# The first group's row maxima move from the attention stage into the last chunk of the projections

## The reference

```python
x = x + 0.5 * ffn(layernorm(x))      # 1024 -> 1024 product with bias, 8 LoRA experts of rank 16, 2 chosen per token
x = x + attn(layernorm(x))
x = x + 0.5 * ffn(layernorm(x))

# attn: 32 query heads of 32, 8 key/value heads, so 4 query heads share one key head
q, k, v = resid @ Wq, resid @ Wk, resid @ Wv
q, k = rope(q), rope(k)
att = einsum('bhgqd,bhkd->bhgqk', q, k) / sqrt(32)      # causal mask, then softmax over the keys
out = (softmax(att) @ v) @ Wo
```

## Time and profile before

| | us |
|---|---|
| three runs | 1561.04, 1562.6, 1565.38 (median 1562.6) |
| the profiled execution, its time | 1565.67 |
| the profiled execution, its span in the trace | 1563.9 |
| TensorE busy in the span | 1511.8 (97%) |
| VectorE, ScalarE, GpSimd busy | 958.9, 569.3, 693.0 |
| mean granted clock of TensorE | 0.984 of full |

### The profile page before, as it was taken

How to read it: one execution, slowest core, us unless ns; L and a number is a source line. 1 busy time by engine, 2 the same in 40 slices (tenths; PEclk the granted TensorE clock), 3 DMA queues, 4 the chain that set the end, 5 groups by cost and what they waited for, 6 DMA issues and landing times. The chain is left out here.

```text
span 1563.9 us, 25960 instructions
## 1 busy us (share of the span) xinstructions
PE 1511.8 (97%) x9184; PEld 1197.1 (77%) x9184; DVE 958.9 (61%) x2727; ACT 569.3 (36%) x1057; POOL 693.0 (44%) x382
## 2 busy tenths in 40 slices
PE   8899998999999969999999999999999999999999
PEld 7899998888888845555555555555479999999998
DVE  6545454656463468888888888888645434343433
ACT  4233232221121125565665565556633212121210
POOL 1222222533343415888888888888612101010100
PEclk9999999999999969999999999999999999999999
DMA  6322324342322262344333333440152212121201
GB/s 232 124 98 110 121 99 148 127 146 81 122 95 81 104 141 63 94 98 97 88 77 76 76 76 89 102 102 28 54 205 79 81 41 81 42 80 40 80 14 41
DMA packets 118773, 145.95 MB, mean 93 GB/s; under 512 B 40976, under 2 KB 77072, under 8 KB 118384
## 3 DMA queue, kind: packets, MB, share of 16 engines
q1 hardware_dynamic: 89920, 120.52, 26.7%
q10 hardware_dynamic: 28736, 23.93, 4.7%
HBM read 95.66 MB, written 53.51 MB: 95 GB/s over the span
## 5 line engine op out<-in xcount | busy, mean ns | idle before, releaser
L1540 ACT ACTIVATE at_probs<-ps 128x512 f32<-128x512 f32 (+1 forms) x640 | 308.1, 557 | 148.3 <-PE ps L1450 147.5
L1609 DVE CUSTOM_DVE_ANT_0 ps<-ps,at_score_mask 128x512 f32<-128x512 f32 (+3 forms) x512 | 289.9, 621 | 50.7 <-PE ps L1439 49.7
L321 POOL TENSOR_TENSOR f_x_ring<-f_x_ring,f_half_bias 128x1024 f32<-128x1024 f32 x32 | 78.1, 2444 | 308.0 <-DVE f_h L607 303.1
L1379 POOL TENSOR_TENSOR at_added<-at_added,at_probs 128x2048 f32<-128x2048 f32 (+1 forms) x60 | 210.8, 3513 | 2.2
L1439 PE MATMUL ps<-at_ks,at_qs 96*128 96x512 f32 (+3 forms) x528 | 185.5, 377 | 16.0 <-DMA at_ks<-scr_k_hi 10.8
L1450 PE MATMUL ps<-at_qs,at_ks 98*128 98x512 f32 (+3 forms) x528 | 178.4, 376 | 3.8 <-ACT at_probs L1540 3.0
L1450 PEld LDWEIGHTS ps<-at_qs,at_ks 98*128 98x128 f32 x528 | 96.6, 193 | 89.9 <-ACT at_probs L1540 50.4
L1465 PE MATMUL ps<-at_probs,at_vs 128*32 128x512 f32 (+3 forms) x1536 | 156.2, 494 | 0.0
L48 PE MATMUL f_ps<-f_wt_hi,f_hT_hi 128*128 128x400 f32 (+1 forms) x384 | 134.4, 350 | 3.3 <-DVE f_hT_lo L611 3.3
L1439 PEld LDWEIGHTS ps<-at_ks,at_qs 96*128 96x128 f32 x528 | 101.4, 197 | 41.7 <-issue 11.2
L50 PE MATMUL f_ps<-f_wt_hi,f_hT_lo 128*128 128x400 f32 (+1 forms) x384 | 131.7, 343 | 0.0
(11 more groups left out here) (164 smaller groups left out, 3159.4 us busy)
## 6 DMA issues: line engine op xcount, KB each, us to landing
at_qs<-scr_q_hi SPq DMA_DIRECT2D x20, 512.0 KB, 5.8
f_x_ring<-in_L_attn_resid SPq DMA_DIRECT2D x16, 512.0 KB, 3.6
x<-f_x_ring SPq DMA_DIRECT2D x16, 512.0 KB, 2.7
early<-x SPq DMA_DIRECT2D x16, 512.0 KB, 3.3
scr_q_hi<-qkv_rope_hi ACTq DMA_DIRECT2D x32, 256.0 KB, 2.0
scr_q_lo<-qkv_rope_lo ACTq DMA_DIRECT2D x32, 256.0 KB, 2.3
scr_ctx<-at_ctxn SPq DMA_DIRECT2D x32, 256.0 KB, 2.4
shared<-scr_ctx SPq DMA_DIRECT2D x16, 512.0 KB, 4.5
```

Source lines behind the costliest of these rows:

```text
L321: pool.tensor_tensor(x_ring[:, u, :], x_ring[:, u, :], half_bias[:], ALU.add).then_inc(bias_added, 1)
L1379: pool.tensor_tensor(added[:, heads, :], first, probs[:, (NU * n + u) % PROBS, heads, :], ALU.add).then_inc(added_done, 1)
L1540: act.activation(probs[:, (NU * n + u) % PROBS, g, cols], score_ps[x % BANKS][:, cols], ACT.Exp, scale=SCALE).then_inc(exp_done, 1)
L1609: dve.tensor_tensor_reduce(out=src, in0=src, in1=mask, scale=1.0, scalar=part_max[:, g, own] if c else -3.0e38, op0=ALU.add, op1=ALU.max, ...
```

## The change

- The 48 row items and the two turns of group 0 are made in the last chunk of `qkv_stage`. PE puts one item behind each of the weight rows c = 1 to 6 of outputs 2 to 9 (six items per output, seven where the turn stands among them). DVE takes the maxima of output o+1's items after its work for output o. Turn B stands ahead of the second value tile. The slots are PSUM banks 0, 1, 6 and 7.
- For that, SP loads the queries and keys of group 0 (and the keys, later the queries, of group 1) within the stage, once the value tiles of the third chunk are done, and writes the rows of maxima of group 0.
- The queries and keys lie where attention will read them: `heads` is an array that both stages hold (it carries the high and low parts of the even chunks' activations before), and group 1's queries lie in the second half of the low query weights, which become `wo`'s low part later. `wq` and `wo` share the pair `wide`.
- The raw weight ring `wkv_raw` shrinks from 4 to 2 slots, and `rot` gets an array of its own.
- ACT takes one exponential of `eps` at the end of `qkv_stage`.
- Attention starts with the eight scores of units 0 and 1 of group 0. The special branches for group 0 are gone; the 49 items of group 1 are spread over units 0 to 8 of group 0 by the rule that holds for the other groups.

```diff
+ROWS = [("row", i, g, c) for i in range(NQ) for c in range(i // QH + 1) for g in range(G)]
+TURN_A, TURN_B = ("turn", 0), ("turn", 1)
+TURN_AT = QH * G + G
...
-    WRAW = 4
+    WRAW = 2
+    ROW_FROM, ROW_SLOTS, PER_O = 2, 4, 6
...
+        hT = sb("hT", [P, 2, KC, HALF], F32R)
+        hT_hi, hT_lo = [[heads[:, part, :, :], hT[:, part, :, :]] for part in range(2)]
...
-        rot = early[:, 3, :].rearrange("p (a n) -> p a n", n=HALF)
+        rot = sb("rot", [P, 2, HALF], F32)
...
+        q_stacks = [hT_hi[0], flat(wq_lo)[:, KC * HALF:].rearrange("p (b n) -> p b n", n=HALF)]
+        behind = hT_lo[0].rearrange("p c n -> p (c n)")
+        k_stacks = [behind[:, n * T:(n + 1) * T] for n in range(3)]
+        spare = flat(wkv_raw)
+        score_mask = spare[:, 0:MASK]
...
+        slot_ps = [ps[:, bank, :] for bank in (0, 1, 6, 7)]
+        items = ROWS[:TURN_AT] + [TURN_A] + ROWS[TURN_AT:] + [TURN_B]
+        number = {it: q for q, it in enumerate(items)}
...
+            own = ROWS[(o - ROW_FROM) * PER_O:(o - ROW_FROM + 1) * PER_O] if ROW_FROM <= o < NO else []
+            return [it for row in own for it in ([TURN_A, row] if row == ROWS[TURN_AT] else [row])]
...
+            def load_negative(half):
+                sp.wait_ge(row_read, number[(TURN_A, TURN_B)[half]] + (ROW_SLOTS + 1))
+                for row, src in enumerate((neg_hi, neg_lo)):
+                    dst = q_stacks[0][KROWS + row:KROWS + row + 1, half * G:(half + 1) * G, :].rearrange("p g t -> p (g t)")
+                    sp.dma_start(dst.bitcast(F32), src).then_inc(neg_loaded, 16)
...
+            sp.wait_ge(v_done, (B * NCH - 1) * TC + 1)
+            for s in range(2):
+                sp.wait_ge(out_stored[s], NCH * NO * 16 + 16)
+            sp.wait_ge(wkv_lo_done, KC)
+            load_queries(0, first_head_loaded)
+            load_keys(0, first_head_loaded)
+            sp.dma_start(score_mask[:, HALF:MASK], consts["score_mask"]).then_inc(first_head_loaded, 16)
+            load_keys(1, rest_loaded)
+            load_negative(0)
+            sp.wait_ge(proj_done, (B * NCH - 1) * NO + KC)
+            load_queries(1, rest_loaded)
+            load_negative(1)
+            sp.wait_ge(rest_loaded, 6 * 16)
+            sp.wait_ge(neg_loaded, 4 * 16)
...
+            def row_item(it):
+                q = number[it]
+                if q == 0:
+                    pe.wait_ge(first_head_loaded, 7 * 16)
+                    pe.wait_ge(v_copied, (B * NCH - 1) * TC + 2)
+                pe.wait_ge(row_read, q + (ROW_SLOTS if it == TURN_B else 1))
+                out = slot_ps[q % ROW_SLOTS]
+                if it[0] == "turn":
+                    pe.transpose(out[0:G * QH, 0:P], row_max[:, it[1], :, :].rearrange("p g q -> p (g q)"),
+                                 ident[:]).then_inc(row_filled, 1)
+                    return
+                _, i, g, c = it
+                keys = row_keys(i, c)
+                pe.matmul(out[:, 0:keys], q_stacks[0][0:KROWS, i // QH * G + g, (i % QH) * P:(i % QH + 1) * P],
+                          k_stacks[0][0:KROWS, c * HALF:c * HALF + keys], start=True, stop=True).then_inc(row_filled, 1)
...
+                        own = [] if more else items_of(o)
...
+                            if 1 <= c <= len(own):
+                                row_item(own[c - 1])
...
+                    if not more and s < 2:
+                        pe.wait_ge(row_read, len(items) - 1 + ROW_SLOTS)
+                    if not more and s == 1:
+                        row_item(TURN_B)
...
+            def negative(half):
+                q = number[(TURN_A, TURN_B)[half]]
+                act.wait_ge(row_filled, q + 1)
+                if half:
+                    act.wait_ge(neg_loaded, 2 * 16)
...
+                    if not more and o and TURN_A in items_of(o):
+                        negative(0)
...
+                    if not more and s == 1:
+                        negative(1)
...
+            act.activation(std[:], eps[:], ACT.Exp)
...
+                if g == NO:
+                    pool.wait_ge(v_done, (B * NCH - 1) * TC + 1)
+                    pool.memset(score_mask[:, 0:HALF], 0.0).then_inc(mask_ready, 1)
+                    pool.wait_ge(mask_ready, 1)
+                    pool.memset(behind[KROWS:KROWS + 2, 0:3 * T].bitcast(F32), 1.0).then_inc(mask_ready, 1)
+                    pool.wait_ge(mask_ready, 2)
+                chunk_step(B - 1, g)
...
+                    if not more:
+                        for it in items_of(o + 1):
+                            row_item(it)
                 rope_sum(b, ch * NO + NO - 1)
+                if not more:
+                    row_item(TURN_B)
...
+        qs = [in_heads(heads[:, 0, :, :].rearrange("p c n -> p (c n)")),
+              in_heads(shared[:].rearrange("p t a c n -> p (t a c n)")),
+              sb("qs2", [P, 2, G, HALF], F32R)]
+        second = in_heads(flat(wo[1])[:, KC * HALF:])
+        ks = heads[0:KROWS + 2, 1, 0:2 * RING, :].rearrange("p c n -> p (c n)").rearrange("p (r t) -> p r t", t=T)
+        def q_stack(n):
+            return second if n == 1 else qs[n % RING]
...
-            load_k(sp, 0, slice(0, HALF), early_loaded)
-            load_q(sp, 0, slice(G, 2 * G), stacks_loaded[0])
-            load_k(sp, 0, slice(HALF, T), stacks_loaded[0])
-            load_v(0)
-            load_rows(0, 0)
-            load(1)
+            for r in range(2):
+                sp.sem_inc(stacks_loaded[r], LOADS - 16)
+                load_v(r)
+            for stored in ctx_stored:
+                sp.sem_inc(stored, 16)
             for n in range(NG):
-                load_rows(n, 1)
                 if n:
+                    load_rows(n, 1)
                     store(n - 1, 0)
                 if n + 2 < NG:
...
-            pe.wait_ge(const_ready, 3)
-            pe.wait_ge(const_loaded, 16)
...
+                if u == 0:
+                    pe.wait_ge(stacks_loaded[n % RING], n // RING * LOADS + LOADS)
...
-            pe.wait_ge(early_loaded, 6 * 16)
+            for u in range(AHEAD):
+                for g in range(G):
+                    scores(0, u, g)
             for n in range(NG):
                 for u in range(NU):
-                    if n == 0 and u in (0, H0):
-                        half = u // H0
-                        for m, it in BEFORE[half]:
-                            if (m, it) == (0, rows[QH * G]):
-                                pe.wait_ge(stacks_loaded[0], LOADS)
-                            slot_item(m, it, it == TURN_A)
-                        for x, items in enumerate(BETWEEN[half]):
-                            scores(0, u + x // G, x % G)
-                            for m, it in items:
-                                slot_item(m, it)
...
-            load_q(act, 0, slice(0, G), early_loaded)
+            act.sem_inc(exp_done, BANKS)
+            act.sem_inc(ctx_copied, 1)
+            for u in range(AHEAD):
+                for g in range(G):
+                    exps(0, u, g)
             for n in range(NG):
                 for u in range(NU):
-                    if n == 0 and u in (0, H0):
-                        negative(0, u // H0)
-                        for x in range(AHEAD):
-                            for g in range(G):
-                                exps(0, u + x, g)
...
-                    if n == 0 and u in (0, H0):
-                        for m, it in BEFORE[u // H0]:
-                            slot_item(m, it)
-                        for items in BETWEEN[u // H0]:
-                            for m, it in items:
-                                slot_item(m, it)
```

More of the change, by code:

```diff
@@ L1010, in low_part, with chunk_step @@
                                    ALU.subtract).then_inc(lo_done, 1)
[L1012 to L1013 removed]
+            def chunk_step(b, g):
                     cols = slice((g // NO) * HALF, (g // NO + 1) * HALF)
```

171 lines of the change are left out of this document (97 added, 74 removed).

## The result

The changed kernel takes 1550.64 us in the median of five runs (1549.88 to 1554.55), the kernel before 1561.55 (1560.73 to 1565.38): ratio 0.9926, 95% interval 0.9913 to 0.9939, so 10.9 us faster. The forecast was 1551.0, inside a range of 1544 to 1557.

The account below looks back on a forecast made before the run. The prediction took TensorE, busy 97% of the span, as the bound. Savings of 31.0 us less losses of 10.3 and 8.9 gave 11.8 saved: 1550.8 against the 1562.6 median, stated as 1551, range 1544 to 1557.

Parts of the forecast that it names:

- Part 1, attention's start: From PE's end of the values to group 0's closing sums: 42.7 us instead of 73.7, a saving of 31.0.
- The hand-over: Between PE's last value matmul and attention's first score: 4.0 us, from a range of 3.3 to 4.2.
- The clock: At attention's start: probably falls in the idle gap, back when unit 0 begins or little later; 1.5 us, bounds 0 and 5.0.
- the denser mix: In group 0 of attention: group 1's 49 items share nine units instead of ten; 1.2 us more at PE's step.
- Part 2, the last chunk: In the last chunk of the projections: items, turns and two new waits on PE lose 10.3 us.
- The first loads' wait: In the last chunk: the first item waits for seven DMAs, 0 to 3 us, taken as 0.5.
- The last maximum: At the last chunk's end: the first value tile waits for DVE's last maximum, about 0.4 us.
- that rival: In the last chunk: DVE's items do not overlap and set the pace, 4.8 us more, 1556; chance 0.13.
- that of the late loads: In the last chunk: first items' loads land 4 us late, 3.5 more plus 2.5 for the clock, 1557; chance 0.08.
- the prediction's sign: In the changed profile: the last chunk's ten outputs 9 to 10 us longer, no PE wait over 1 us for DVE.
- Part 3, the ring of two: At the projections' start: first tile's turn 6.4 us later, plus 2.5 for restarting at half clock; 8.9 lost.
- one of the signs of being wrong: At the projections' start: PE turning the first tile before 290 would mean the ring costs little.

Follow-up runs that it names:

- busy_scores: The changed kernel with 14 unread matmuls behind the last value tile and one behind each of attention's first eight scores; 1548.76 us, 0.991 of the kernel before.
- short_maxima: The changed kernel with the last chunk's 48 row maxima on VectorE reading 16 keys each, score matmuls whole; 1551.78 us, 0.9926 of the kernel before.
- ring_alone: The kernel before with only the raw weight ring cut from 4 to 2 slots; 1571.58 us, 1.006 of the kernel before.
- heads_low: The changed kernel with `heads` moved to the low end of memory, `early` and `shared` to the high end; 1554.04 us, 0.9944 of the kernel before.

## Why the prediction held, point by point

- **Part 1, attention's start** (42.7 predicted, 42.83 measured). The hand-over is right (4.0, measured 3.89). The clock was mis-sized: 1.5 taken, 3.05 by busy_scores. The text had the clock back when unit 0 begins or a little later; it came back 6.9 us behind the start of unit 0, where half clock is dear. The sum was kept by two terms that were too dear, read in busy_scores at full clock: 4.2 for the eight scores, measured 3.55, and 31.8 + 1.2 from unit 0 to the sums, measured 32.35, so the denser mix costs 0.55 and not 1.2 (group 1 takes 31.80 from its first score, 612.72, to 644.52). So errors of 1.3 and 1.55 us cancel, and the near hit of this part is luck too.
- **Part 2, the last chunk** (10.3 predicted, 10.7 with the value tiles left out). The items' price is right within a fifth: 8.8 predicted for the 48 matmuls, 10.08 measured. All four sizes were put too low, those of 128 columns the most (0.1, measured 0.122). The turns were put at 0.3 each and cost about half of that. The first loads' wait (0.5) did not come, and PE took the first item without idle time. The last maximum was right (0.4, measured 0.43). VectorE does not pace the chunk, by short_maxima: that rival falls, and so does that of the late loads. The outputs grew by 10.7 us and not by 9 to 10, as the prediction's sign had it.
- **Part 3, the ring of two** (8.9 predicted). The front costs 9.2, but the ring's part of it is 6.85 by ring_alone: 5.58 for the first turn (6.4 predicted, with 5.5 as the lower bound) and 1.48 between the first and the second (2.5 for the clock). The other 2.35 is not in ring_alone; heads_low gives back 1.88 of it from the third turn on, so nearly all of it is the place of `heads`, which the prediction did not have at all. The near hit of this sum is luck. By the letter one of the signs of being wrong came true: TensorE turned the tile at 288.38, before 290. But the first transposes came 3.57 us sooner in this execution than in the earlier trace rows; counted from them it is 24.76 us where the sign's 290 stands for 22.8, so the ring is not cheap and the sign was badly put. Besides, the text held that a tile normalized ahead of ACT's eighth piece is what the order forbids. True of this order, but two moved operations undo it and show that the loss is not one of the ring.
- **The sum.** In us from the first transposes: + 9.20 in front, + 10.71 in the last chunk, + 0.16 in the value tiles, - 30.85 from their end to the sums, - 0.30 behind, that is 11.08 saved against 11.8 predicted. The mechanisms of the three parts held; the closeness of the total owes something to errors that cancelled inside the parts.

## What to carry to other kernels

A smaller ring need not cost time, though the wait shows up at once: look at which short operations stand behind the ring's transfers in each engine's order, and move them out, on every engine that the next tile passes through (here ScalarE's, then GpSimd's). When a stage starts with work that a slower engine feeds, the clock can fall inside the start, not only at the border, and a few filler matmuls between the real ones, whose results nobody reads, can keep it up where those at the border alone do not (3.05 us against 0.12 here). Ask too where the half clock falls: it cost next to nothing while TensorE waited for ScalarE, and 0.44 us per microsecond behind that. Compare profiles from a landmark behind the parts that the change does not touch: here one such stage alone differed by up to 4.7 us between executions.

## What was unexpected of the hardware

Where a tensor lies in SBUF changes the pace of dense matmuls. Those of 512 columns came every 0.234 us instead of 0.227 when they read their moving operand from a tensor at the high end (`heads`) and the stationary one from the query weights at the low end, and again when the stationary one was high (`shared`) and the moving one low. The two key outputs of such a chunk, whose stationary operand is the key weights, show the same 0.233. With 256 columns it is otherwise: the value tiles, whose stationary operand is `heads`, took 11.56 us in the first and third chunk of the changed kernel against 11.67 in the second. I have no mechanism for it.
